# Second part's rows scaled ahead in one block, and down weights read where they lie: the seam of an attention and expert kernel rearranged

## The reference, cut to what matters

```python
logits = x @ gate_w
top_val = jnp.max(logits, axis=-1, keepdims=True)
top_id = jnp.argmax(logits, axis=-1)
xs = x * jax.nn.sigmoid(top_val)
g = jnp.einsum('th,ehi->eti', xs, rt_gate)      # 8 experts, 128 -> 256
u = jnp.einsum('th,ehi->eti', xs, rt_up)
y = jnp.einsum('eti,eih->eth', jax.nn.silu(g) * u, rt_down)
routed = jnp.einsum('eth,te->th', y, one_hot(top_id))
shared = swiglu(x, sh_gate, sh_up, sh_down)
```

## Time and profile before

| | us |
|---|---|
| median of 3 executions | 827.63 (826.82 to 829.07) |
| the profiled execution, its own time | 832.66 |
| its span, first to last instruction | 830.8 |
| TensorE busy | 783.3 (94% of the span) |
| VectorE, ScalarE, GpSimd busy | 669.4, 549.1, 261.2 |

### The profile page before, as it was taken

The page is one execution under the profiler, slowest core; times in us unless marked ns, Lnnn a source line. Parts: engine busy times, 40 slices in busy tenths (PEclk is TensorE's granted clock), DMA queues, the critical chain, the costliest instruction groups (busy, mean ns, idle before and its releaser), DMA issues.

```text
span 830.8 us, 14920 instructions
## 1 busy us (share of the span) xinstructions
PE 783.3 (94%) x4464; PEld 631.7 (76%) x4464; DVE 669.4 (81%) x1810; ACT 549.1 (66%) x975; POOL 261.2 (31%) x301
## 2 busy tenths in 40 slices
PE   5899997897789899899999999999999999999997
PEld 4788776776789899877777777777777777777775
DVE  5888889886775688778888898888888888888774
ACT  3577667695323335377777678777777867877765
POOL 2332322666278254121331232132133123211000
PEclk9999999999899999999999999999999999999999
DMA  6346784552534343100000000000000000000000
GB/s 172 87 119 192 201 241 135 171 167 75 155 100 123 108 111 96 44 22 4 26 26 0 25 25 19 6 26 25 0 25 25 0 25 25 19 7 13 13 1 26
DMA packets 91176, 55.80 MB, mean 67 GB/s; under 512 B 13439, under 2 KB 87799, under 8 KB 90999
## 3 DMA queue, kind: packets, MB, share of 16 engines
q1 hardware_dynamic: 75440, 41.29, 17.5%
q0 software_dynamic: 4096, 8.40, 3.5%
q10 hardware_dynamic: 11591, 5.50, 2.4%
HBM read 32.23 MB, written 22.94 MB: 66 GB/s over the span
## 4 chain that ended last, share of the span: by engine, by line
PE 74%; DVE 11%; ACT 7%; issue 4%; another core or an unknown queue 2%; DVEq 0%; DMA 0%; POOL 0%; ACTq 0%; SPq 0%
PE PS L1088 7%; PE PS L841 7%; PE PS L1110 7%; PE PS L1090 7%; PE PS L1089 7%; PE PS L1112 6%; PE PS L1111 6%; PE PS L856 6%; PE PS L1097 3%; PE PS L1099 3%; PE PS L1041 3%; PE PS L864 2%; DVE xn L1169 2%; PE PS L1024 2%
## 5 line engine op out<-in xcount | busy, mean ns | idle before, releaser
L798 ACT ACTIVATE sil<-PS,b_in_c 128x512 f32<-128x512 f32 x256 | 162.2, 685 | 91.9 <-PE PS L1097 87.0
L1562 DVE TENSOR_TENSOR sil_l<-sil,sil_h 128x512 fp32r<-128x512 f32 x256 | 164.8, 685 | 48.6 <-ACT sil_h L806 48.6
L543 POOL TENSOR_TENSOR ve<-mv,eps 128x4 f32<-128x4 f32 x64 | 19.2, 299 | 444.1 <-DVE mv L1163 443.0
L806 ACT ACTIVATE sil_h<-sil 128x512 fp32r<-128x512 f32 x224 | 128.9, 631 | 0.0
L1110 PE MATMUL PS<-sil_h,wout_l 128*128 128x512 f32 x256 | 118.8, 464 | 1.7 <-DVE sil_l L1562 1.6
L1088 PE MATMUL PS<-x4T_h,win_l 128*128 128x512 f32 x256 | 102.5, 400 | 0.9 <-ACT sil L798 0.4
L1112 PE MATMUL PS<-sil_h,wout_h 128*128 128x512 f32 x256 | 100.7, 393 | 0.0
L1111 PE MATMUL PS<-sil_l,wout_h 128*128 128x512 f32 x256 | 100.2, 391 | 0.0
L1090 PE MATMUL PS<-x4T_h,win_h 128*128 128x512 f32 x256 | 99.9, 390 | 0.0
L1089 PE MATMUL PS<-x4T_l,win_h 128*128 128x512 f32 x256 | 99.8, 390 | 0.0
L1546 DVE TENSOR_SCALAR dec<-PS,b_in_c 128x512 bf16<-128x512 f32 x128 | 95.4, 745 | 3.9 <-PE PS L1090 2.1
(11 more groups left out here) (178 smaller groups left out, 1594.7 us busy)
## 6 DMA issues: line engine op xcount, KB each, us to landing
x_sorted<-zeros SPq DMA_DIRECT2D x4, 1280.0 KB, 6.8
xs_in<-x_sorted SPq DMA_DIRECT2D x20, 256.0 KB
y_sorted<-yo ACTq DMA_DIRECT2D x18, 256.0 KB
X<-in_x SPq DMA_DIRECT2D x16, 256.0 KB
rows<-xn SPq DMA_DIRECT2D x16, 256.0 KB
out<-res SPq DMA_DIRECT2D x16, 256.0 KB
ctxT<-in_ctx_t SPq DMA_DIRECT2D x16, 240.0 KB
ctx_rows<-in_ctx_kv SPq DMA_DIRECT2D x16, 240.0 KB
```

The lines of the kernel that those rows point to most:

```text
L798: act.activation(tile(sil[p % 2], c, W), bank(2 * (p % 2) + c), ACT.Silu, bias=b_in_c[:, 2 * p + c:2 * p + c + 1]).then_inc(t_silu, 1)
L806: act.activation(tile(sil_h[p % 2], c, W), tile(sil[p % 2], c, W), ACT.Copy).then_inc(t_hi, 1)
L1562: dve.tensor_tensor(tile(sil_l[p % 2], c, W), tile(sil[p % 2], c, W), tile(sil_h[p % 2], c, W).bitcast(F32), ALU.subtract).then_inc(t_lo, 1)
```

## The change

Six edits. (1) The eight scales of the second part are no longer strewn between GpSimd's calls: GpSimd scales groups 8 to 11 as soon as the scores are there, ahead of the places, and ScalarE scales groups 12 to 15, one in each of the units 1 to 4 (`scale_late`). The 32 calls follow each other. (2) VectorE no longer copies the down weights. TensorE reads EXPERTS itself, once for each unit, and takes the weights at a run-time address in WD. (3) TensorE counts the second part after three quarters of the shared expert's down products and not after `r_turn(0, 0)`, and VectorE reads both counts where TensorE left them, without copying them. (4) The copy of unit 0's first weights moves from "pack" behind the choice in "all". (5) The second part's `a_pack` moves from the end of unit 0 to the start of unit 5. (6) ScalarE computes the scores before it evacuates unit 0's turned rows.

```diff
-                if k >= HG + XB:
-                    pool.wait_ge(late_in[v], 16)
-                else:
-                    pool.wait_ge(k_in[v], 16 * (k // XB + 1))
+                pool.wait_ge(k_in[v], 16 * (k // XB + 1))
...
-                if h and t % G == 2 and k + 1 < end:
-                    scale(k + 1)
                 if 0 < k < HG:
                     pool.wait_ge(k_act, k)
+                elif k >= HG + XB:
+                    pool.wait_ge(k_late, k - HG - XB + 1)
...
             pool.wait_ge(scored, 2)
-            scale(HG)
+            for k in range(HG, HG + XB):
+                scale(k)
             pool.wait_ge(placed, 2)
...
+            def scale_late(k):
+                act.wait_ge(scored, 2)
+                act.wait_ge(late_in[k % XB], 16)
+                rows = rows_of(k)
+                for j in range(G):
+                    i = act.activation(tile(rows, j), tile(rows, j), ACT.Identity,
+                                       scale=SCORE[:, k * G + j:k * G + j + 1])
+                i.then_inc(k_late, 1)
...
                 if route == "all":
+                    score(1)
                     r_evac_x(0, 0)
-                    score(1)
...
+                if 1 <= r <= XB:
+                    scale_late(HG + XB + r - 1)
...
 -                if m is not None:
+                if route == "all":
+                    s_down(2, 1)
+                    a_count(1)
+                    s_down(3, 1).then_inc(s_y_ps, 1)
+                    pe.wait_ge(a_k1, NG)
+                    r_turn(0, 0)
+                elif m is not None:
                     s_down(2).then_inc(s_y_ps, 1)
                 if route == "all":
-                    pe.wait_ge(a_k1, NG)
-                    r_turn(0, 0)
-                    a_count(1)
                     pe.wait_ge(w_exp, 48)
                     pe.wait_ge(routed, 1)
+                    first_experts.extend(experts_of(pe, 0))
...
-                                      tile(wd_now[v][t], c), start=(c == 0), stop=(c == FC - 1))
+                                      cols(WD, experts[2 * v + t] * (FC * P) + c * P, P), start=(c == 0), stop=(c == FC - 1))
...
-            def a_counts():
-                dve.wait_ge(r_cnt, 2)
-                dve.tensor_copy(et(counts[:, 0:HBS[1] * E]), COUNTS_IN[1][1].rearrange("p (t e) -> p e t", e=E))
-                dve.tensor_copy(ahead[:, 0:HBS[1] * E], COUNTS_IN[1][0]).then_inc(r_read, 1)
-                dve.wait_ge(r_read, 2)
...
+                if h:
+                    dve.wait_ge(r_cnt, 2)
+                    step(dve.tensor_tensor_scan(up, keeps[h], COUNTS_IN[1][1], 0.0, ALU.mult, ALU.add))
...
+                ah = COUNTS_IN[1][0] if h else ahead
...
-                for t in range(n):
-                    dve.tensor_copy(wd_now[v][t], cols(WD, experts[2 * v + t] * (FC * P), FC * P))
...
-            a_pack(1)
-            dve.wait_ge(routed, 2)
             for r in range(1, NR - 1):
+                if r == HR // 2:
+                    a_pack(1)
+                    dve.wait_ge(routed, 2)
```

More of the change, by code:

```diff
@@ L108, in program @@
         W0 = sb("W0", [P, P])
-        WQT = WA[:, C_RANK:C_RANK + P]
+        WQT = sb("WQT", [P, P])
         WKT = sb("WKT", [P, P])
@@ L858, in r_gate_up, with s_down @@
                 i.then_inc(r_gu_ps, 1)
-            def s_down(start):
-                for j in (start, start + 1):
+            def s_down(start, n=2):
+                for j in range(start, start + n):
                     for c in range(FC):
@@ L876, in a_count @@
                 pe.matmul(COUNTS_IN[h][0], before[:, :], some, start=True, stop=True)
-                pe.matmul(COUNTS_IN[h][1], all_ones[:, :], some, start=True, stop=True).then_inc(r_cnt, 1)
+                if h:
+                    pe.matmul(et(COUNTS_IN[h][1]), all_ones[:, :], some.rearrange("p (t e) -> p e t", e=E),
+                              start=True, stop=True).then_inc(r_cnt, 1)
+                else:
+                    pe.matmul(COUNTS_IN[h][1], all_ones[:, :], some, start=True, stop=True).then_inc(r_cnt, 1)
             def merge_weights():
@@ L1034, in _, with r_down @@
             pe.wait_ge(a_rows, 16 * NG)
-            def r_down(r, v):
+            def r_down(r, v, experts):
                 pe.wait_ge(r_act, 2 * r + v + 1)
@@ L1041, in r_down, with r_body @@
                         i = pe.matmul(tile(bank(6), 2 * v + t), tile(ract[v], FC * t + c),
-                                      tile(wd_now[v][t], c), start=(c == 0), stop=(c == FC - 1))
+                                      cols(WD, experts[2 * v + t] * (FC * P) + c * P, P), start=(c == 0), stop=(c == FC - 1))
                 i.then_inc(r_y_ps, 1)
-            def r_body(r, u, end=False):
+            def r_body(r, u, was, now=None, end=False):
                 q = 2 * r
+                if not end:
+                    coming = experts_of(pe, r + 1)
                 if not first(r):
-                    r_down(r - 1, 1)
+                    r_down(r - 1, 1, was)
                 if not end:
@@ L1053, in r_body @@
                         r_turn(r + 2, u)
+                if now is None:
+                    now = experts_of(pe, r)
                 if isinstance(r, int):
@@ L1062, in r_body @@
                     pe.wait_ge(r_y, r)
-                r_down(r, 0)
+                r_down(r, 0, now)
                 if end:
-                    return
+                    return now
                 r_gate_up(q + 3, 1, r + 1, 1 - u)
+                return now, coming
             r_gate_up(1, 1, 0, 0)
-            for r in range(NR - 1):
-                r_body(r, r % 2)
+            now, coming = r_body(0, 0, None, first_experts)
+            for r in range(1, NR - 1):
+                if r == HR - 1:
+                    pe.wait_ge(routed, 2)
+                now, coming = r_body(r, r % 2, now, coming)
                 if r == FIRST_EARLY + 2:
@@ L1074, in _ @@
                     c_turn_prob(0)
-            r_body(NR - 1, 1, end=True)
-            r_down(NR - 1, 1)
+            now = r_body(NR - 1, 1, now, coming, end=True)
+            r_down(NR - 1, 1, now)
             c_turn_x(1)
@@ L1261, in a_body @@
                     a_choose(3)
-                    r_weights(0, 1, experts_of(dve, 0))
+                    dve.wait_ge(w_exp, 48)
+                    dve.wait_ge(routed, 1)
+                    now = experts_of(dve, 0)
+                    r_weights(0, 0, now)
+                    r_weights(0, 1, now)
                 if route == "pack":
@@ L1387, in a_first_slots @@
                 up = upto[:, 0:n * E]
-                step(dve.tensor_tensor_scan(up, keeps[h], counts[:, 0:n * E], 0.0, ALU.mult, ALU.add))
+                if h:
+                    dve.wait_ge(r_cnt, 2)
+                    step(dve.tensor_tensor_scan(up, keeps[h], COUNTS_IN[1][1], 0.0, ALU.mult, ALU.add))
+                else:
+                    step(dve.tensor_tensor_scan(up, keeps[h], counts[:, 0:n * E], 0.0, ALU.mult, ALU.add))
                 step(dve.tensor_scalar(tiles_i, et(up)[:, :, n - 1], float(P - 1), None, ALU.add))
@@ L1398, in a_slots @@
                 n = HBS[h]
-                up, sl, ah, ld, oh = (a[:, 0:n * E] for a in (upto, slot, ahead, lead, onehot))
+                up, sl, ld, oh = (a[:, 0:n * E] for a in (upto, slot, lead, onehot))
+                ah = COUNTS_IN[1][0] if h else ahead
                 step(dve.tensor_tensor(et(sl), et(up), first_slot.unsqueeze(2).to_broadcast([P, E, n]), ALU.add))
@@ L1520, in _ @@
                     c_norm4(0)
-                r_second(r, now, coming)
-                now = coming
+                r_second(r, coming)
                 if r == HR + 1:
@@ L1534, in _ @@
                     c_rows4(0)
-            r_mul(NR - 1, 0, now)
-            r_mul(NR - 1, 1, now)
+            r_mul(NR - 1, 0)
+            r_mul(NR - 1, 1)
             c_x4_low(0)
```

36 lines of the change are left out of this document (14 added, 22 removed).

## The result

The changed kernel took 820.14 us (median of 4 runs, 818.77 to 821.39), the kernel before 827.32 us on the same chip (4 runs, 826.82 to 829.07): a ratio of 0.9906, interval 0.9895 to 0.9918, so 7.2 us less. The forecast was 821.4 us, which is 6.2 us less. The profiled execution took 820.4 us, span 818.4. As will be seen, this result does not hold on every chip.

What follows compares the result with a forecast made beforehand. TensorE bounds the steady units and trees; only the seam, where VectorE is late, and a few waits can give time. Terms -3.8 - 2.0 - 0.4 = -6.2 us, from 827.63 to 821.4; forecast range 818 to 824.5, outer ends 815.5 and 827.5.

Steps and rivals of the forecast that it cites:

- Counting and scales on VectorE: Ahead of POS: counting edits -1.1 us, scales beside VectorE +2.25; POS at 230.05 instead of 228.90.
- Pair 0 of unit 2: In the seam: TensorE starts this pair at 234.5 instead of 236.60, -2.1 us.
- unit 3: Behind the seam: begins 3.8 us earlier, 2.1 from the pair before and 1.7 from the full clock.
- Units 3 to 9: Stretch up to unit 10's turn: removing down-weight copies saves 2.0 us, bounds 0 and -2.0.
- the pieces of 0.34: TensorE's losses per unit, 2.0 us in all, read as waits for r_act behind VectorE's down-weight copies.
- the 2.12 us for yo: TensorE's one wait for ScalarE's yo ahead of unit 10's turn; left in place, no gain counted.
- GpSimd's calls: 32 calls take 41.8 us, ending at 272.4; unit 10's load has 5.2 us until the turn, no wait.
- TensorE's registers: Each unit's register load, arithmetic and instructions, 0.86 us, counted as 0; rival of all exposed, about 838, chance 0.09.
- List of experts: Moved to unit 5, about 2 us of VectorE work there; counted as 0, bound +1.
- ScalarE's four scales: 4 times 0.41 us in a unit, hidden while TensorE is busy: 0; uncovered, up to 1.6 in each of four units.
- The wait of 1.65: Units 10 to 19, at 344.86: ends with a VectorE product behind down-weight copies; their going gives -0.4 us.
- the forecast's seam: Stretch up to unit 3: VectorE's line shortens, pair 0 of unit 2 -2.1 us, then -1.7 to unit 3.

Runs made afterwards that it cites:

- the last run: The changed kernel with half a GpSimd scale (128x256) behind every second call of the second part: 832.7 us against 827.9 of the kernel before (1.0056).
- two variants of it: The changed kernel with VectorE's down-weight copies back (851.9 us, 1.0207), and with the second part's list of experts made in unit 0 again (851.8 us, 1.0206).

## Why the prediction was right, and on which chips only

**Counting and scales on VectorE** (forecast 1.15 us later at POS): right. From the first step of the choice on the logits to the end of POS it took 13.37 us before (215.53 to 228.90) and 14.60 after (212.60 to 227.20), 1.23 more. The four scales cost 0.88, 0.40 and, for two of them beside the copies, 1.67 us: 0.74 each where I took 0.75. The scan from PSUM took 0.68, no more than from SBUF (0.69). The page "SBUF — State Buffer" of the Trainium skill, section "Who interferes with whom", says that of a VectorE and a GpSimd instruction which contend, the one that issues first has the shared ports for the whole instruction and the other is blocked. The steps that ended just behind a scale agree; most scales cost less than their own 1.04 us, since a part of the scale was over when the step began.

**Pair 0 of unit 2** (234.5) **and unit 3** (3.8 us sooner): right. Less the 2.53 us ahead of the seam, unit 2's pair came 2.6 us sooner and in 1.95 us, unit 3's 4.3 us sooner. Not foreseen: the first pair of unit 0 now takes 3.75 us at the lower of TensorE's two clock levels (granted clock 0.50 from 219.6 to 223.2, which is 1.2 GHz). TensorE had waited 2.27 us for the choice ahead of 216.43; in the last run, where this wait was 1.45 us, the pair took 2.02. That the wait is the cause was not tested.

**Units 3 to 9** (2.0 us): the step that was mis-sized and misread. They lost 4.15 us in the profile of before and lose nothing now (273.87 - 237.30 = 36.57, where the records need 36.6). I read the pieces of 0.34 as down-weight copies behind a "remote" signal, and left the 2.12 us for yo as ScalarE's. Both lie among late increments of TensorE, and the changed kernel's profile on the chip of the result has none. If before has none there either, the 2.0 us were not there to be won. The profile of before speaks for that: in units 10 to 18, behind the calls but with all the copies, TensorE waited for a product once, 0.34 us at 314.33. In the run with the copies back they made TensorE wait 0.26 us ahead of the hold. What they cost on the chip of the result is open.

**GpSimd's calls** (41.8 us, unit 10's rows in time): right, 41.0 us. The margin was worth naming: it was some 0.5 us, and with calls of 54 us the wait was 12.07. With whole scales between the calls (48.0 us) the wait would be about 6 us on such a chip, by these numbers; that was not run there. So edit 1 is what lets the other edits count where the increments are on time.

**TensorE's registers** (0): right, though 28 times 0.13 and 0.49 for the extras are 4.1 us of sequencer time, and not under 4. In the profile after, 156 register instructions of 76 ns (median) stand in the units, and no wait stands ahead of a down product but the one for yo at 339.51. **List of experts**: in unit 5 it cost TensorE nothing; in unit 0 it made it wait 1.08 us at 235.42, just over the 0.4 to 1 us expected. **ScalarE's four scales** (0): right, TensorE has no wait in units 1 to 4. **The wait of 1.65**: 1.25 after, the 0.4 forecast.

**The total** is partly luck. The 6.2 us were counted on a profile of before whose increments come late, and set against medians of a chip on which, as far as its profile shows, they do not. Of the terms the 2.0 us for units 3 to 9 are doubtful there, and some 1.8 us (0.8 ahead of the seam and 1.0 behind unit 10) stand in the spans where the sum had nothing.

**What the prediction did not have** is the hold. The rows showed it: VectorE's 10.4 us of idling for "remote", which I took for an unnamed signal to be lived with. No rival asked what comes of it when the pauses between the calls go. On such a chip this decides the sign: 16 us for edit 1 (851.4 against 835.1), 1.8% in all. The changed kernel itself was timed on one chip of this kind; two variants of it took 852 us on a second, and a third shows the late increments only in kernels with fewer or spaced calls. Where the hold is absent the forecast's seam holds, as far as the one chip that timed both kernels shows. Open is what differs between the chips, by what path GpSimd's calls hold TensorE's increments, and how long a pause must be: a scale of 1.0 us behind every fourth call left increments up to 5.6 us late, an operation of 1.0 to 1.3 us behind every second at most 1.1. No kernel here is shown to beat the one before on both kinds of chip; beside the changed kernel none was timed on both.

## What to carry to other kernels

Where many waits end with "remote" and the increments are TensorE's, look what GpSimd issues beside them before calling the wait a fact of life; an edit that packs such calls closer may turn it into the bound. Time such an edit on more than one chip: here the same two kernels stand at 0.991 on one and 1.018 on another. And a gain ahead of a transfer is only worth what the transfer's own chain leaves of it, so keep both lines in the sum, TensorE's and that of the calls.

## What the runs showed of the hardware

- GpSimd's indirect DMA calls, 1.27 us apart, can hold TensorE's semaphore increments: 22.8 us late beside 20 calls, freed together 3.4 us after the last of them, and up to 3.9 us late behind five. TensorE then issues single matmuls 0.7 to 2.1 us apart. The long hold was seen on two chips, late increments on three; on the chip of the result increments came 0.01 us behind their matmuls beside the same 32 calls, and on that of the last run too.
- A scale of GpSimd (128x512) made VectorE instructions of 0.17 to 0.43 us take 0.69 to 1.27, and each ended 0.02 to 0.28 us behind the scale. A reduction of 0.29 us and a product with one input in PSUM (0.67) were not stopped.
- A small power operation of GpSimd (128x4) took 1.0 to 1.3 us between calls.
